# A fused RWKV-style attention and feed-forward kernel: where the feed-forward weights are prepared in the first three steps

## The reference, cut to what matters

```
xn  = layernorm(x)
xk, xr, xv, xg = xn + (xn shifted by one token - xn) * time_maa_{k,r,v,g}
k, r, v = xk @ Wk.T, xr @ Wr.T, xv @ Wv.T ;  g = silu(xg @ Wg.T)
per head (32 of 16 channels), chunks of 64 tokens:
    att = (r_c @ k_c) * w_mat
    y_c = att @ v_c + r_c @ state * wb
    state = ws * state + (k_c * wk) @ v_c
x   = x + (groupnorm(y) * gamma + beta) * g @ Wo.T
D   = gelu(float16(layernorm(x)) @ W0.T + bias0)       # W0: 2048 x 512, float32
x   = x + float16(float16(D) @ W1.T + bias1)           # W1: 512 x 2048, float32
```

## Time and profile before

| | us |
|---|---|
| median of 3 runs | 2140.63 (2139.34 to 2142.56) |
| the profiled execution | 2144.0 |
| its span, first to last instruction | 2142.2 |
| PE busy | 2052.8 (96%) |
| DVE busy | 1812.5 (85%) |
| ACT busy | 1303.7 (61%) |
| POOL busy | 388.8 (18%) |

### The profile page before, as it was taken

How to read it: one execution, slowest core, us unless ns; L and a number is a source line. 1 busy time by engine, 2 the same in 40 slices (tenths; PEclk the granted TensorE clock), 3 DMA queues, 4 the chain that set the end, 5 groups by cost and what they waited for, 6 DMA issues and landing times.

```text
span 2142.2 us, 57711 instructions
## 1 busy us (share of the span) xinstructions
PE 2052.8 (96%) x23836; PEld 1463.0 (68%) x23836; DVE 1812.5 (85%) x3607; ACT 1303.7 (61%) x2054; POOL 388.8 (18%) x330
## 2 busy tenths in 40 slices
PE   4678999999999999999999999999999999999988
PEld 4556677777667777766777766777776667677655
DVE  6888898888889888888989888898988889898751
ACT  7554566776556677655667665666766566676532
POOL 1111112111111211111121211112221111222110
PEclk8889999999999999999999999999999999999999
DMA  6544678887777888776788877768887777787666
GB/s 208 187 143 159 190 216 236 242 233 197 224 227 219 229 239 241 200 219 211 215 242 239 233 197 224 226 211 240 239 235 202 220 224 219 231 239 226 197 214 233
DMA packets 401221, 467.33 MB, mean 218 GB/s; under 512 B 242112, under 2 KB 279488, under 8 KB 400960
## 3 DMA queue, kind: packets, MB, share of 16 engines
q1 hardware_dynamic: 399328, 463.44, 72.7%
q10 hardware_dynamic: 1632, 0.21, 0.1%
HBM read 316.24 MB, written 25.17 MB: 159 GB/s over the span
## 4 chain that ended last, share of the span: by engine, by line
PE 84%; DVE 3%; ACT 2%; SPq 2%; issue 2%; DMA 1%; ACTq 0%; DVEq 0%
PE F L944 20%; PE F L973 20%; PE B L771 10%; PE B L924 8%; PE sc L771 7%; PE YT L799 6%; PE YT L771 3%; PE sc L833 3%; PE YT L854 2%; PE YT L897 2%; PE YT L873 2%; DMA y<-ygT 1%; PE YT L857 1%; SPq L1761 1%; SPq L1748 0%
## 5 line engine op out<-in xcount | busy, mean ns | idle before, releaser
L944 PE MATMUL F<-xT,ring 128*128 128x256 f16 x4096 | 483.9, 275 | 10.4 <-DMA ring<-w_dram 5.3
L973 PE MATMUL F<-ring,hT 128*128 128x512 f16 x2016 | 475.2, 379 | 1.4 <-ACT hT L1538 1.4
L944 PEld LDWEIGHTS F<-xT,ring 128*128 128x128 f16 x4096 | 398.3, 99 | 75.3 <-issue 7.0
L1538 ACT ACTIVATE hT<-F,b,f_rho 128x256 f16<-128x256 f32 x512 | 260.8, 561 | 122.1 <-PE F L944 121.7
L973 PEld LDWEIGHTS F<-ring,hT 128*128 128x128 f16 x2016 | 189.7, 98 | 200.5 <-ACT hT L1538 2.4
L1705 POOL TENSOR_TENSOR Shl<-S,Shl 128x512 f16<-128x512 f32 x128 | 156.6, 1224 | 748.7 <-ACT Shl L1503 748.7
L771 PE MATMUL B<-mix,WT 128*128 128x256 f16 x2304 | 270.7, 275 | 0.0
L1503 ACT ACTIVATE Shl<-S 128x512 f16<-128x512 f32 x128 | 80.9, 632 | 291.1 <-PE YT L873 162.3
L771 PEld LDWEIGHTS B<-mix,WT 128*128 128x128 f16 x2304 | 224.4, 99 | 36.8 <-DVE gT L1197 0.3
L252 DVE SCALAR_TENSOR_TENSOR mixf<-dx,maa,xnT 128x256 f32<-128x256 f32 x512 | 238.8, 528 | 0.5 <-PEq L517 0.3
L1167 DVE TENSOR_TENSOR att<-att 128x512 f16<-128x512 f32 x256 | 178.9, 740 | 13.2 <-ACT att L1497 13.1
(11 more groups left out here) (169 smaller groups left out, 2925.4 us busy)
## 6 DMA issues: line engine op xcount, KB each, us to landing
ring<-w_dram SPq DMA_DIRECT2D x512, 512.0 KB, 4.4
kx<-kT SPq DMA_DIRECT2D x96, 256.0 KB, 3.7
rx<-rT SPq DMA_DIRECT2D x96, 256.0 KB, 4.4
xa<-in_L_attn_x SPq DMA_DIRECT2D x32, 512.0 KB, 7.4
vbd<-vN SPq DMA_DIRECT2D x256, 64.0 KB, 3.1
x<-in_L_attn_x SPq DMA_DIRECT2D x32, 512.0 KB, 6.1
out<-x SPq DMA_DIRECT2D x31, 512.0 KB, 4.0
ring<-in_L_ffn_W SPq DMA_DIRECT2D x10, 512.0 KB, 8.5
```

Source lines behind the costliest of these rows:

```text
L944: mm = eng.matmul(F[:, j % 2, i * BT:(i + 1) * BT], ring[:, use % RING, i, a * C + kk * P:a * C + (kk + 1) * P], xT[:, :, kk, :], start=(k ...
L973: mm = eng.matmul(F[:, t, :], hT[:, k, rows(t)], ring[:, use % RING, i, a * C:(a + 1) * C], start=(k == 0 and a == 0), stop=(k == NH - 1 a ...
L1538: eng.activation(hT[:, k, :], F[:, j % 2, i * BT:(i + 1) * BT], ACT.Gelu, bias=b0[:, k:k + 1], scale=f_rho[:, j:j + 1]).then_inc(s_h, 1)
```

## The change

The sixteen pieces are spread over three steps. Step 0 still handles the eight pieces of W0, but three of them among K and R (after K1, R0, R1), then V0, V1, G0, G1 and sc2. Step 1 handles four pieces of W1 (V0, G0, G1, sc2), and step 2 the last four (K0, K1, R0, R1). The scales of W0 are made in two parts, three pieces first at the head of step 0 (its matmul is the first instruction of PE there) and five after R1. The largest sum of W1 is taken earlier in step 1. On SP each place is loaded with its W1 piece right after its W0 piece has been written, which makes SP wait for that write, and step 2 gets the writes of pieces 12 to 15 among its transfers.

```diff
-PREPARED_AT = (("R1", "V0", "V1", "G0", "sc1", "G1", "sc2", "sc3"),
-               ("V0", "V1", "X1", "G0", "sc1", "G1", "sc2", "sc3"))
+PREPARED_AT = (("K1", "R0", "R1", "V0", "V1", "G0", "G1", "sc2"), ("V0", "G0", "G1", "sc2"), ("K0", "K1", "R0", "R1"))
+FIRST_AT = (0, PIECES, PIECES + 4)
+SCALED = (0, 3, PIECES, 2 * PIECES)
...
-    return PIECES * n + PREPARED_AT[n].index(place) if n < 2 and place in PREPARED_AT[n] else None
+    return FIRST_AT[n] + PREPARED_AT[n].index(place) if n < len(PREPARED_AT) and place in PREPARED_AT[n] else None
...
-    piece_mean = sc[:, 0, 0:PIECES]
+    piece_mean = (Y[:, 1, 0:3], sc[:, 0, 0:5], sc[:, 0, 0:1])
...
-        eng.wait_ge(s_ones, 1)
-        eng.wait_ge(s_kl, 2 * k + 2)
         if k == 0:
-            eng.wait_ge(s_psq, PIECES)
-            sums = f_sum[:, 0:PIECES]
+            eng.wait_ge(s_ones, 1)
+        else:
+            eng.wait_ge(s_kl, 2 * k)
+        if k < 2:
+            eng.wait_ge(s_psq, SCALED[k + 1])
+            sums = f_sum[:, SCALED[k]:SCALED[k + 1]]
...
@@ pe_step
         if att_n:
+            if n == 0:
+                pe_piece_mean(eng, 0)
             pe_mixed(eng, n, 0)
             pe_K(eng, n, 0)
+            pe_prepare(eng, n, "K0")
...
             pe_K(eng, n, 1)
+            pe_prepare(eng, n, "K1")
...
             pe_R(eng, n, 0)
+            pe_prepare(eng, n, "R0")
...
             if n < 2:
-                pe_piece_mean(eng, n)
+                pe_piece_mean(eng, n + 1)
@@ dve_step
             if att_n and early:
                 mix_lo(eng, n, 2)
+                dve_prepare(eng, n, "K0")
+            if n == 1:
+                dve_piece_most(eng)
...
             dve_row_mean(eng, n)
+            dve_prepare(eng, n, "K1")
...
         if att_n:
-            if n == 0:
-                dve_piece_scale(eng, 0)
-            if n == 1:
-                dve_piece_most(eng)
             dve_R_lo(eng, n, 0)
+            dve_prepare(eng, n, "R0")
             dve_R_lo(eng, n, 1)
-            if n == 1:
-                dve_piece_scale(eng, 1)
             dve_prepare(eng, n, "R1")
+            if n < 2:
+                dve_piece_scale(eng, n + 1)
@@ act_step
             act_K_hi(eng, n, 0)
+            act_prepare(eng, n, "K0")
...
             act_K_hi(eng, n, 1)
+            act_prepare(eng, n, "K1")
...
             act_R_hi(eng, n, 0)
+            act_prepare(eng, n, "R0")
             act_mix_hi(eng, n, 3)
             act_R_hi(eng, n, 1)
+            act_prepare(eng, n, "R1")
...
-            act_prepare(eng, n, "R1")
@@ sp_step
             sp_kx(eng, n)
             sp_k_tokens(eng, n)
+        if n == 2:
+            sp_prepared(eng, 12)
+            sp_prepared(eng, 13)
+            eng.wait_ge(s_stash[4], 32)
+            sp_weights(eng, 4)
+        if n == 0:
+            sp_prepared(eng, 0)
+            sp_raw(eng, 1, 0)
...
             sp_rx(eng, n)
         if n == 0:
-            sp_prepared(eng, 0)
+            sp_prepared(eng, 1)
+            sp_raw(eng, 1, 1)
+        if n == 2:
+            sp_prepared(eng, 14)
+            sp_prepared(eng, 15)
...
         if n == 1:
-            for j in range(PIECES):
+            for j in range(4):
                 sp_prepared(eng, PIECES + j)
-            for j in range(PIECES):
+            for j in range(4):
                 eng.wait_ge(s_stash[j], 32)
-                if j < RING:
-                    sp_weights(eng, j)
+                sp_weights(eng, j)
```

More of the change, by code:

```diff
@@ L701, in pe_piece_mean @@
             sums = f_most[:, :]
-        eng.matmul(piece_mean[:, 0:1] if k else piece_mean, mean_of, sums, start=True, stop=True).then_inc(s_pall, 1)
+        eng.matmul(piece_mean[k], mean_of, sums, start=True, stop=True).then_inc(s_pall, 1)
     def dve_piece_most(eng):
@@ L709, in dve_piece_scale @@
         eng.wait_ge(s_pall, k + 1)
-        at = slice(PIECES, PIECES + 1) if k else slice(0, PIECES)
-        most = piece_mean[:, 0:1] if k else piece_mean
+        at = slice(SCALED[k], SCALED[k + 1]) if k < 2 else slice(PIECES, PIECES + 1)
         for i in range(POW2_PER):
-            dve_power(eng, i, s_pscl, POW2_PER * k, most, f_rho[:, at], f_scl[:, at])
+            dve_power(eng, i, s_pscl, POW2_PER * k, piece_mean[k], f_rho[:, at], f_scl[:, at])
     def piece_scale(q):
-        k = q // PIECES
-        at = q if q < PIECES else PIECES
+        k = sum(q >= first for first in SCALED[1:3])
+        at = min(q, PIECES)
         return f_scl[:, at:at + 1], POW2_PER * k + POW2_PER - 1
@@ L725, in pe_prepare @@
         j = q % PIECES
-        eng.wait_ge(s_raw[j], 16 * (n + 1))
+        eng.wait_ge(s_raw[j], 16 * (q // PIECES + 1))
         if due(q):
@@ L730, in pe_prepare @@
             for b in range(G):
-                if n == 0:
+                if q < PIECES:
                     src = raw_piece(j)[:, C * i + P * b:C * i + P * b + P]
@@ L744, in act_prepare @@
         eng.wait_ge(s_ptr, q + 1)
-        eng.wait_ge(s_psq, PIECES * n + q % PIECES + 1)
+        eng.wait_ge(s_psq, q + 1)
         eng.activation(parts_of(q % PIECES)[:, :, 0:C], F[:, :, :], ACT.Identity, scale=scale).then_inc(s_phi, 1)
@@ L796, in pe_V @@
             eng.wait_ge(s_yi if t else s_y, NT * n)
+        else:
+            eng.wait_ge(s_pscl, 1)
         for i, (a, b) in enumerate(PASSES):
@@ L809, in pe_yT @@
         if n == 1:
-            eng.wait_ge(s_pscl, POW2_PER + 1)
+            eng.wait_ge(s_pscl, 2 * POW2_PER + 1)
         for t in range(NT):
@@ L821, in pe_scores @@
             if n == 0:
-                eng.wait_ge(s_pscl, 1)
+                eng.wait_ge(s_pscl, POW2_PER + 1)
             if due(n) and not y_by_dma(n - 1):
@@ L1324, in dve_step @@
                 mixing(G)
+            if n == 0:
+                dve_piece_scale(eng, 0)
             if ahead:
@@ L1845, in sp_step @@
         if n == 0:
-            sp_prepared(eng, 1)
+            sp_prepared(eng, 2)
+            sp_raw(eng, 1, 2)
         if late and n < nb + 2:
@@ L1858, in sp_step @@
         if n == 0:
-            sp_prepared(eng, 2)
+            sp_prepared(eng, 3)
+            sp_raw(eng, 1, 3)
         if ff:
@@ L1877, in sp_step @@
         if n == 0:
[L1878 to L1881, removed]
             for j in range(4, PIECES):
                 sp_prepared(eng, j)
-                sp_raw(eng, 1, j - 1)
-            sp_raw(eng, 1, PIECES - 1)
+                sp_raw(eng, 1, j)
         if n == 1:
-            for j in range(PIECES):
+            for j in range(4):
                 sp_prepared(eng, PIECES + j)
-            for j in range(PIECES):
+            for j in range(4):
                 eng.wait_ge(s_stash[j], 32)
-                if j < RING:
-                    sp_weights(eng, j)
+                sp_weights(eng, j)
         if ff:
```

## The result

The changed kernel takes 2149.79 us (median of 6 runs, 2146.98 to 2156.16) where the kernel before takes 2140.63 (6 runs, 2138.52 to 2142.56). The ratio is 1.0044, with an interval of 1.0034 to 1.0054, so it is slower by 0.44%, more than the 0.2% that can be told from no change. The prediction had said 2146.9, with 2143 to 2150 as the forecast's own range, so the result is 2.9 above the forecast and 0.2 inside that range.

A forecast was written before the change was run, and what follows sets the result against it. PE was taken to bound the whole span, a chain through DVE steps 0, 1 and early step 2. +5.4 - 7.5 + 8.4 = +6.3 on 2140.6 gave 2146.9 us, range 2138.5 to 2151.5.

The forecast's parts named there:

- Step 0, K and R: Step 0: PE idles 3.5 us before the piece between R's halves; `vw` and `dx` come 8.3 us later.
- The head of step 0: Step 0: the small matmul ahead of K waits for a memset, 0.4 us, bounded by 0 and 1.
- Step 0, the rest: Step 0 after `dx`: three pieces instead of five, earlier by 2.9 us, so the step ends 5.4 late.
- Step 1: Step 1: shorter by 7.5 us, 3.5 of it from the earlier largest sum, the rest from pieces gone.
- Step 2, the late write: Step 2: the first GELU waits for piece 14's write; longer by 8.4 us, 3.8 if never late.
- Step 2, the clock: Step 2: R's first half at the low clock behind transposes, about 1.2 us more, left out of the sum.
- The sum: Steps 0 to 2 together: +5.4 - 7.5 + 8.4 = +6.3 us, nothing moved from step 3 on; chance 0.45.
- No late write: Rival, step 2: writes land faster or the queue has drained, step 2 costs 3.8; +1.7, 2142.3 us; chance 0.18.
- it does what it says: Rival, steps 0 and 2: waits and idle time take in the moved pieces; -8.0, 2132.6 us; chance 0.14.
- The clock holds: Rival, step 0: the clock stays up through PE's 3.5 us idle stretch; +3.8, 2144.4 us; chance 0.15.
- More than forecast: Rival: two writes land a microsecond later each and R runs at 4.70; +9 to +10, 2150 us; chance 0.08.

The follow-up runs named there:

- e5: Changed kernel with no piece between the halves of R in step 0, one before the scores instead: 2143.82 us, ratio 1.0009 to the kernel before.
- e8: The changed kernel once more, no edit, with a second profile: 2151.54 us, ratio 1.0040 to the kernel before.
- e6: Changed kernel with the first three scales moved behind the row variance of step 0, after POOL's memsets: 2149.87 us, ratio 1.0033 to the kernel before.
- e3: Kernel before with only the largest sum of W1 taken earlier, before the rsqrt steps of step 1: 2139.05 us, ratio 0.9991.
- e11: e3 once more, no edit: 2139.97 us, ratio 0.9994 to the kernel before.
- e1: Changed kernel with the wait for piece 14's write moved from the first GELU to the fifth: 2144.09 us, ratio 1.0009 to the kernel before.
- e2: Changed kernel with SP issuing piece 14's write ahead of the wait for piece 12 and of `rx`: 2144.87 us, ratio 1.0016 to the kernel before.
- e4: e3 with W1's pieces over steps 1 and 2 as in the changed kernel, step 0 as before: 2145.89 us, ratio 1.0017 to the kernel before.

## Why the prediction was right, point by point

- **Step 0, K and R.** Predicted: `vw` at 72.2, `dx` at 82.5, an idle stretch of PE of 3.5. Found: 72.68, 83.09, 3.65. The mechanism is the one told (one `F`, its round in series with R), and e5 shows it alone. R's second half was put at 4.0 between 2.78 and 4.70; it took 3.90 and, in e8, 4.57.
- **The head of step 0.** The small matmul ahead of K was put at 0.4, between 0 and 1. K starts 0.75 later in both profiles of the changed kernel. The three scales, counted at nothing by the prediction, delayed piece 0 by about 1.1 (e8 against e6).
- **Step 0, the rest.** Predicted 2.9 earlier. `dx` is 8.0 late from the step's start and its end 4.9, so 3.1.
- **Step 1.** Predicted 7.5 shorter, found 7.7 and in e8 6.4. The early sum was put at 3.5; at `vw` it is worth 3.4, but at the end of the step 2.7 and 2.2 (e3, e11), since other waits on DVE take some of it; so of the 7.5 about 1 less came from the sum than was added up, and the first profile's 7.7 met the total partly by its milder clock.
- **Step 2, the late write.** Predicted: 8.4 longer, 3.8 without the late write, so 4.6 for it. Found 9.2 and 8.9; e1 takes 5.1 of this away and e2 4.5, and 4.1 are left for the pieces. The write was issued 29.9 us into the step, 0.4 earlier than forecast, but it landed 4.4 after its issue and not 3.2 as by the earlier trace rows: the median of ten writes was used for one that is issued while the DMA engines are nearly full. e2, where it took 5.1 ahead of `rx`, shows that the place behind `rx` is not the reason.
- **Step 2, the clock.** The 3.8 for the pieces was 4.8 less 1 for a long idle stretch of PE that would be gone. It wasn't gone: it moved from 5.54 us behind V to 5.73 before the transposes of piece 13 (5.59 in e8). The transposes behind V then ran at full rate, 0.60 and 0.63 for 1.09 and 1.06, and the first up projection took 1.91 for 3.31, and R's first half ran slowly instead, 3.26 and in e8 4.56 for 2.78. This is the term of 1.2 that the prediction left out, but it stands behind an idle stretch, as in the earlier trace rows, so no run shows whether transposes alone would have caused it. In the changed kernel it seems to cost nothing, since the write ends later: R was 1.3 slower in e8 and step 2 0.3 shorter. But that the forecast's 3.8 agrees with the 4.1 left in e1, where no write hides it, is in part luck.
- **The sum.** Predicted +6.3. The medians differ by 9.2 (9.1 in the second comparison). Sign, places and the two main mechanisms were right, and the size was 3 us short. Where the 3 us lie is known from two profiles alone. By e8, whose profile adds up to 9.4, the terms that were too small are step 0 with its start (6.9 for 5.4, from the low clock and the head), step 1 (6.4 gained for 7.5) and step 2 (8.9 for 8.4), 3.1 in all. The first profile comes to 7.05 with the start, nearer to the forecast mostly by its clock phase.
- **The rivals.** "No late write" fell with the row of the table load, "it does what it says" with both places. "The clock holds" fell in both profiles, at 3.65 and at 4.63 us of idle time: part of what follows ran slow each time, though in the first over a third of the price was spared (1.66 + 3.90 against 1.94 + 4.70, where the full clock takes 1.04 + 2.78). "More than forecast", +9 to +10 and 2150, had a chance of 0.08, and its number is the one that came: the medians are 9.2 and 9.1 apart. Of its two reasons R at 4.70 came nearly in full in e8 (4.57), and of the two writes that of piece 14 landed 1.2 later than forecast, while that of piece 12 took 3.0. The rest of the difference is the shorter gain of step 1 and the head of step 0, which it didn't name.

## What to carry to other kernels

A piece of side work that goes through one shared buffer can cost its whole round, from PE over ACT and DVE back to PE, where the main work stands in order behind it, as between the halves of R, while the piece at K1 cost little; so before such a piece is put into an idle stretch, ask whether the main work can pass it. When work is spread over more steps, follow the last hand-over and not the work: here one write behind another wait in its own queue cost about 5 us, as much as the four pieces it belonged to, and splitting its wait by the first real use gave that back. And a change of 0.4% needs at least two profiles of the changed kernel before its terms are added up, since one stretch at the lower clock differed by over a microsecond between two profiles of the same kernel, and the landing of one write by 2.5 us between two kernels that issue it at the same place.

## What the runs showed of the hardware that was not expected

- A tiny instruction of DVE (128x3, int32) takes 1.73 us instead of 0.17 while POOL clears 128x2048 float32 values in 1.82, and ends with the memset. The one that reads from PSUM, beside the same memset, took 0.15, and statistics of 128x512 values 0.69 in e6, as without a memset. So it is not DVE as a whole that stands still.
- The same 24 matmuls behind eight transposes and 5.3 to 5.7 us of idle time took 3.26, 4.56 and 4.90 us in three runs. The first two are the changed kernel itself, so the program alone does not set which, and one profile of a stretch at the low clock is one draw.
- A write of 512 KB that takes 3.2 us from issue to landing in the median took 4.3 to 4.7 behind the three transfers of `rx` in five profiles and 6.9 in a sixth (e4), and 5.1 ahead of them, right behind two other writes (e2). From 203 to 212 us the mean busy share of the DMA engines was 0.94 in the changed kernel and 0.98 in e2. That this load is the cause is argued, and was not tried alone.
